# A masked key layout for the second attention layer: written by ScalarE in the routing stage, where GpSimd wrote it between two expert tiles

## The reference, cut to what matters

```python
k = (key @ Wk + bk).reshape(B, Nk, NUM_HEADS, HEAD_DIM).transpose(0, 2, 1, 3)
attn = jnp.einsum('bhqd,bhkd->bhqk', q, k) * SCALE
...
for e in range(num_experts):
    h = x @ w1[e]
    a, g = jnp.split(h, 2, axis=1)
    y = jax.nn.silu(a) * g @ w2[e]
    out = jnp.where((max_ind == e)[:, None], y, out)
out = out * max_prob
```

## Time and profile before

| | us |
|---|---|
| median of 3 runs | 599.5 |
| the runs | 599.04, 599.5, 603.42 |
| profiled execution | 607.98 |
| its span, first to last instruction | 605.3 |

### The profile page before, as it was taken

The page is one execution under the profiler, slowest core; times in us unless marked ns, Lnnn a source line. Parts: engine busy times, 40 slices in busy tenths (PEclk is TensorE's granted clock), DMA queues, the critical chain, the costliest instruction groups (busy, mean ns, idle before and its releaser), DMA issues.

```text
span 605.3 us, 10237 instructions
## 1 busy us (share of the span) xinstructions
PE 511.0 (84%) x3068; PEld 371.4 (61%) x3069; DVE 422.1 (70%) x809; ACT 291.0 (48%) x513; POOL 251.8 (42%) x322
## 2 busy tenths in 40 slices
PE   8888899897898799897999999947598779459994
PEld 3446667666784278786888888833354445335562
DVE  5299778887735887496377732325989898678992
ACT  1256645353553276482456632302354545427884
POOL 4446253344300312032021210048257878628996
PEclk9799969799598889897999999989699999688999
DMA  7930000100166156552466201023000000000111
GB/s 211 297 132 1 18 18 2 35 1 1 35 207 209 54 157 197 181 190 75 136 206 234 95 26 35 9 62 95 1 1 1 1 1 1 0 0 1 36 35 69
DMA packets 35163, 46.40 MB, mean 77 GB/s; under 512 B 2765, under 2 KB 25305, under 8 KB 35129
## 3 DMA queue, kind: packets, MB, share of 16 engines
q1 hardware_dynamic: 30856, 39.02, 20.0%
q0 software_dynamic: 1680, 4.59, 2.7%
q10 hardware_dynamic: 2592, 2.36, 1.1%
HBM read 38.36 MB, written 7.60 MB: 76 GB/s over the span
## 4 chain that ended last, share of the span: by engine, by line
PE 49%; DVE 29%; POOL 8%; issue 8%; ACT 3%; DVEq 1%; DMA 0%; POOLq 0%; ACTq 0%
PE s_tile L978 16%; PE bank L999 8%; DVE s_max L1470 5%; PE bank L713 4%; DVE p_sum L1484 4%; PE bank L829 3%; DVE probs L1475 3%; PE bank L988 3%; DVE stats L1408 2%; DVE ew L1430 2%; PE s_tile L1072 2%; DVE ew_lo L1740 2%; POOL probs_t L616 2%; DVE xn L1430 2%; PE bank L890 2%
## 5 line engine op out<-in xcount | busy, mean ns | idle before, releaser
L506 POOL TENSOR_TENSOR probs<-probs,p_rcp 128x1024 f32<-128x1024 f32 x32 | 60.9, 1906 | 99.8 <-DVE p_rcp L1487 99.8
L978 PE MATMUL s_tile<-ew_hi,xs_hi 128*128 128x512 f32 x144 | 60.9, 423 | 7.6 <-DVE xs_lo L1750 5.1
L742 PE MATMUL bank<-ident,probs 128*128 128x128 f32 x256 | 39.7, 305 | 24.8 <-POOL probs L506 21.7
L978 PE MATMUL s_tile<-ew_hi,xs_lo 128*128 128x512 f32 x144 | 58.5, 406 | 0.0
L978 PE MATMUL s_tile<-ew_lo,xs_hi 128*128 128x512 f32 x144 | 58.2, 404 | 0.0
L564 POOL TENSOR_TENSOR token_now<-token_of,carried 128x1 uint32<-128x1 uint32 x17 | 3.8, 224 | 126.4 <-PE bank L962 126.4
L1758 DVE TENSOR_TENSOR probs_t<-s_tile,probs_t 128x512 f32<-128x512 f32 x36 | 24.8, 690 | 44.8 <-PE s_tile L978 43.4
L1169 ACT COPY probs_t<-bank 128x512 f32<-128x512 f32 x64 | 34.9, 589 | 43.7 <-PE bank L742 43.5
L742 PEld LDWEIGHTS bank<-ident,probs 128*128 128x128 f32 x256 | 32.3, 156 | 36.8 <-POOL probs L506 27.9
L1470 DVE TENSOR_REDUCE s_max<-s_tile 128x16 f32<-128x1024 f32 x32 | 38.4, 1200 | 21.4 <-PE s_tile L726 21.2
L1740 DVE TENSOR_TENSOR ew_lo<-ew,ew_hi 128x512 fp32r<-128x512 f32 x64 | 45.2, 762 | 10.3 <-ACT ew_hi L1256 9.4
(11 more groups left out here) (227 smaller groups left out, 1324.6 us busy)
## 6 DMA issues: line engine op xcount, KB each, us to landing
ew<-in_L_ffn_w SPq DMA_DIRECT2D x32, 512.0 KB, 5.0
ew<-in_L_ffn_w SPq DMA_DIRECT2D x8, 1024.0 KB, 5.3
slots_y<-xn ACTq DMA_DIRECT2D x18, 128.0 KB, 3.7
x_res<-in_x SPq DMA_DIRECT2D x4, 512.0 KB, 6.2
token_rows<-ew SPq DMA_DIRECT2D x4, 512.0 KB, 3.1
out_rows<-x_res SPq DMA_DIRECT2D x3, 512.0 KB, 3.0
w<-in_L_xattn_W SPq DMA_DIRECT2D x2, 512.0 KB, 9.3
ew<-in_L_ffn_w_gate SPq DMA_DIRECT2D x1, 1024.0 KB, 12.6
```

What stands on the lines that cost most here:

```text
L506: nc.gpsimd.tensor_tensor(p, p, p_rcp[:, i, :].unsqueeze(2).to_broadcast([P, H, M]), ALU.mult).then_inc(s["p_norm"], 1)
L742: last = nc.tensor.transpose(t_bank[c][:, P * j:P * j + P], probs[:, i % 2, at:at + P], ident[:])
L978: last = nc.tensor.matmul(o[:], x, w, start=(k == 0 and n == 0), stop=(k == DK - 1 and n == 2))
```

## The change

Layer 1's spread leaves POOL's list and goes to ACT's. There it is eight ACTIVATE instructions (Identity, with a column of `group_mask` as the scale), one for each block and head group, each over the four batches: 128 x 256 elements again, with an output of four pieces of 64. They stand behind `keys(1, t_bank)`. The last of them raises `a_k` once more, to 2 * DK + 1, and PE's first scores of layer 1 wait for that instead of `p_kbd`. ACT now waits for its own `a_k` and for `t_s` of layer 0. Layer 0's spread stays on POOL.

```diff
-            def spread_keys(l):
-                pool.wait_ge(a_k, DK * l + DK)
+            def spread_keys():
+                pool.wait_ge(a_k, DK)
                 for b in range(B):
                     for m in range(DK):
                         nc.gpsimd.tensor_tensor(
...
-            spread_keys(0)
+            spread_keys()
...
-            pool.wait_ge(att[0]["t_s"], NT)
-            spread_keys(1)
...
-            pe.wait_ge(p_kbd, 2 * DK * B)
+            pe.wait_ge(a_k, 2 * DK + 1)
             scores(1, 0, 0)
...
             keys(1, t_bank)
+            act.wait_ge(a_k, 2 * DK)
+            act.wait_ge(att[0]["t_s"], NT)
+            for m in range(DK):
+                for h in range(GH):
+                    last = nc.scalar.activation(k_bd[:, m, :, M * h:M * h + M],
+                                                k_t[:, m, :].rearrange("p (b s) -> p b s", b=B), ACT.Identity,
+                                                scale=group_mask[:, h:h + 1])
+            last.then_inc(a_k, 1)
```

## The result

The median fell to 597.43 us (592.02 to 603.6, 16 runs). The kernel before, run beside it, had 603.9 us (599.04 to 608.16, 16 runs): more than the 599.5 of the three runs that the prediction started from. The ratio is 0.988 with a 95% interval of 0.9853 to 0.9907, so the change gains 1.2%, or 7.2 us of 603.9. The medians lie 6.5 us apart; the ratio compares only runs in the faster of the two states that an execution can fall into, which leaves out 600.97 and 603.6 us of those after.

The account below looks back on a forecast made before the run. PE bounds the kernel (busy 84%), and POOL's spread makes it wait through DVE. A 4.01 us wait plus 3.13 us of lowered clock gives 7.1 us off 599.5: 592.4 us, range 590.0 to 599.0.

Parts of the forecast that it names:

- its own case: Expert tiles: the whole 7.1 us gain also appears in the timed runs, 590.5 to 594.5 us; chance 0.60.
- the smaller hold: Rival at tile 6: DVE was held less in the timed runs; gain 0 to 4 us, 597.5 us; chance 0.25.
- the base: Starting time of the timed runs before the change: median 599.5 us of three, from which 7.1 us was subtracted.
- The hold: DVE between tiles 5 and 6: POOL's back-to-back products stop a two-SBUF-input L1740, 5476 ns against 687.
- The pause: PE at tile 6 waits for the rows' late lower part; without the wait it goes on 4.01 us earlier.
- what is late next: Tile 6 without the wait: rows, weights, DVE's sequencer and POOL's gather all in time; tightest slack 0.2 us.
- The clock's part: PE at tile 6: clock falls to 0.50 after the wait, costing 3.13 us more, which the change saves.
- The copies on ACT: Routing stage: eight ACTIVATEs of 0.51 us, 4.1 us in all, hidden in idle time; nothing on the path.
- the cover: ACT's idle time before the first rows, 11.29 us; gone only if the eight ACTIVATEs take over about 10 us.
- the slower rival: ACT before the first rows: ACTIVATEs, dear through four-piece output, delay rows and all expert tiles; 605.5 us; chance 0.05.
- The first rows: ACT's start on the expert tiles' rows: still at 211 us after the change.

Follow-up runs that it names:

- experiment 11: Kernel before, unedited, profiled once more: one execution of 601.59 us, 188.60 us from first rows to first result gather.
- experiments 3: Kernel before with four of layer 1's eight POOL products: ratio to before 0.9934, 184.95 us from first rows to first result gather.
- experiment 4: Kernel before with twelve POOL products instead of eight in layer 1: ratio to before 0.9993, 190.83 us from first rows to first result gather.
- experiment 8: Kernel before with POOL waiting for each of layer 1's products before the next: ratio to before 0.9911.
- Experiment 6: Kernel before with layer 1's spread at its old place on POOL, as eight tensor_scalar with one tensor input: ratio to before 0.9894.
- experiment 5: Kernel after with each of ACT's eight copies made four times, 32 in all: ratio to before 0.9928.
- experiments 2: Kernel before with layer 1's eight POOL products moved behind tile 4's gather instead of tile 8's: ratio to before 0.9946.
- 7: Kernel before with layer 1's eight POOL products moved behind tile 5's gather: ratio to before 0.995.
- experiments 1: Kernel after without ACT's eight copies, so layer 1's keys are not spread at all: ratio to before 0.9898.
- 12: Kernel after, unedited, profiled and timed once more: ratio to before 0.9885, 183.24 us from first rows to first result gather.
- 9: Kernel after with layer 0's spread moved to ACT as well: ratio to before 0.9854.
- 10: Kernel after with POOL's bias-row products in layer 0's first three batches waiting two batches longer: ratio to before 0.9841.

## Why the prediction was right

**The number** has luck in it. 597.43 us lies outside the 590.5 to 594.5 that the prediction gave to its own case, and inside the 595.5 to 599.5 of the smaller hold, a case that the traces contradict. The mechanism came as forecast and the gain is right as a ratio; that the time still fell into the full range is owed to its width, which covered an error in the base that no term of the sum allowed for.

**The hold** (4.79 us on one instruction) is confirmed by its absence after, by its return to 5469 ns in experiment 11 and by its length in experiments 3 and 4. That it is the row of products and not the place alone is experiment 8. The rival in which the timed runs were held less had a gain of 4 us at most. Against it stand both traces of before, which have the whole hold, and the ratio, whose interval begins at 5.6 us. As the start may have a share in that ratio, experiments 6 and 8 are the cleaner witnesses: there the work is still on POOL, the profiled start was late (first s_max at 26.3 and 25.1 us), only the long hold is gone, and the ratios are worth 6.4 and 5.4 us. Their intervals are wide, though (2.2 to 10.6 and 2.8 to 8.0).

**The pause** (4.01 us) was sized rightly: PE waited 3.9 us in both traces of before and not at all after. My reading of what is late next held as well: nothing was. PE's only other wait from 258 to 292 us was one of 0.2 us for L1764.

**The clock's part** (3.13 us) is the term that one execution couldn't size. It was 3.1, then 1.6 in the repetition, and 2.1 behind the longer pause of experiment 4 (4.86 - 2.75). With 1.6 the change is worth 188.60 - 183.24 = 5.4 us, with 3.1 it is 6.87. The timed 7.2 us, with an interval of 5.6 to 8.9, takes in the second; the first lies just below it. So that 7.1 met 7.2 this closely is partly chance: the prediction took the dearer of two costs of the clock, and the timed runs may hold a share of the early start.

**The copies on ACT** were priced at 4.1 us and took 3.3: 0.49 each instead of 0.51, and neighbours overlap. On the path they were worth nothing, as I had said, and experiment 5 puts the cover at 11.2 us (I had said about 10). ACT's idle time left was 7.6 us where I had about 7. The four-piece output, the only open point of the slower rival, costs next to nothing: 492 ns, beside 484 for a plain one that reads PSUM.

**The first rows** came at 205.15, not at 211. Of these 5.90 us 5.06 passed ahead of 27 us, before any changed instruction.

**The base** was the largest error: three runs with a median of 599.5, sixteen with 603.9. The runs of before span 9.1 us. The difference of 4.4 us is of the size of what the early clock gives or takes, but no trace of before has the early start, so its cause stays open. The prediction noted that three runs lay 4.4 us apart and still took their middle as it stood; the profiled execution at 607.98 had spoken against it.

**What decides who waits is only partly settled.** Shown is this: a row of four, eight or twelve products without a gap kept VectorE's instruction to the row's end when that instruction had begun just ahead of it (experiments 3 and 4 and both traces of before). POOL's gather just ahead of the row isn't what held it: the L1740 before the long one ran beside that gather in its usual 0.69 us. With a gap (8), or as tensor_scalar (6), the two engines alternate. Experiment 6 began as the kernel before did, POOL's first instruction 0.35 us behind the start of a 128 x 512 L1745 (268.76 and 269.11 us); yet L1745 took its 0.68 us and POOL's 0.68 instead of 0.47. So there it was POOL which waited. That the number of tensors read is the reason, and not another difference of the two forms, is argued. Open is also why VectorE got in at the eighth product in experiments 2 and 7 (which then took 1.05 and 1.59 us against 0.60) and in the kernel before only behind it.

The Trainium skill has a rule for this that I had not used, on the page "SBUF — State Buffer", section "SBUF: two separate sides": a VectorE instruction with two SBUF inputs and a GpSimd instruction that reads SBUF exclude each other, and whichever starts first keeps the shared ports for its whole instruction. The traces agree that it is a full block and no sharing of bandwidth (5476 ns for 687 ns of work), and the alternation in experiments 6 and 8 looks like it. They disagree on two points: L1740 had started 0.33 us ahead of the first product and L1742 0.31 us ahead, and both lost (counted from the end of the instruction before it, L1740 was still 0.24 us ahead); and the block lasted not one of GpSimd's instructions but four, eight or twelve. By the rule alone L1740 would have lost nothing, and the change would have been worth nothing. The measurement decides.

## What to carry to other kernels

In a group of like instructions compare the longest with the median; a single one many times longer, beside a row of GpSimd products on SBUF, points to a hold. It costs what stands behind it on VectorE's list and reaches the engine that sets the pace. Put such a row where nobody waits for VectorE, break it with a wait between the products, write it as tensor_scalar with one tensor input, or give it to an engine with idle time of known length. Here the last three left no pause at all (stages within 0.3 us), the first left 0.4 to 1.3 us. Before a difference of 1% is read from two profiles, cut both at the same instructions, so that what varies ahead of the change isn't booked to it, and within the stretch compare the places where the clock falls: here one of them alone moved five stages by 1.6 us.

## What the runs showed of the hardware

- The granted clock in the first 27 us differs between kernels whose instructions there are the same, by 3.3 to 5 us: first s_max at 21.8 or 21.9 us in after and in experiments 1 and 12, at 25.1 in 8, and at 26.2 to 26.9 in before and in 2 to 7 and 9 to 11 (9 alone has other instructions there).
- The same pause doesn't always cost the same clock. After the wait of 2.5 us ahead of tile 4's matmuls the clock fell to 0.50 in nine executions (both of before, both of after, 1, 2, 6, 8 and 10: 12 matmuls in 4.26 to 4.61 us) and stayed at 1.00 in five (3, 4, 5, 7 and 9: 3.02 to 3.04 us). That is 1.6 us of stage, as much as some of the differences between experiments. After 3.9 us at tile 6 it fell in both traces, for 5.49 + 0.83 or 4.37 + 0.44 us.
- The wait of 2.5 us ahead of tile 4 is still in the kernel after. The L1746 that ends it begins behind loads, branches and register work of DVE's sequencer (L281 to L284, 242.9 to 244.6 us on the chain). The wait and the clock that falls behind it make 4.1 us, beside the 6.9 that this change won in its stage.
- One long product (2.36 us) also holds a VectorE instruction with a single SBUF input, to 2.18 us from 0.41.
- Copies with a column as scale cost ACT 0.41 to 0.42 us each when they stand in a row (3.30 us for 8, 13.30 for 32).
